# Perceiver block on one core: the feed-forward layer turned so that inner features lie on partitions, its layer norm taken apart, and the self attention's value products put ahead of the next scores

## The reference

```python
x = x + attn(layernorm(x), WQ, WK, WV, WO)        # scores, causal mask, softmax, values, WO
def ffn(x, W_fc, ln_w, ln_b, W_proj):
    h = einsum('btd,hd->bth', x, absmean(W_fc))   # 512 -> 2048, weights in {-1, 0, 1}
    h = gelu(h, approximate=False)
    h = layernorm(h, ln_w, ln_b)                  # over the 2048 inner features
    return einsum('bth,dh->btd', h, absmean(W_proj))
x = x + ffn(layernorm(x), ...)
```

## Time and profile before

| what | value |
|---|---|
| median of 3 runs | 1124.6 us (1123.21 to 1125.88) |
| profiled execution, its own time | 1122.38 us |
| its span, first to last instruction | 1120.2 us |
| granted TensorE clock, mean | 0.969 |
| busy PE, DVE, ACT, POOL | 956.8, 688.4, 453.0, 441.0 us |

### The profile page before, as it was taken

The page is one execution under the profiler, slowest core; times in us unless marked ns, Lnnn a source line. Parts: engine busy times, 40 slices in busy tenths (PEclk is TensorE's granted clock), DMA queues, the critical chain, the costliest instruction groups (busy, mean ns, idle before and its releaser), DMA issues.

```text
span 1120.2 us, 22904 instructions
## 1 busy us (share of the span) xinstructions
PE 956.8 (85%) x7466; PEld 809.4 (72%) x7466; DVE 688.4 (61%) x1352; ACT 453.0 (40%) x972; POOL 441.0 (39%) x572
## 2 busy tenths in 40 slices
PE   0898879888788888779798988889869999999996
PEld 0787757676676767668688887778647888888885
DVE  3587666766766767764545554655556665565554
ACT  2565445554455545444323232434363322322321
POOL 1354444444444444410212111111016767667663
PEclk9999999999999999979799998999879999999999
DMA  5532233221223222411534443334331111101101
GB/s 167 156 92 55 71 89 95 89 60 59 84 83 92 72 80 73 158 38 40 170 116 112 114 136 95 107 108 108 107 118 38 58 34 52 57 29 57 57 19 50
DMA packets 96769, 95.11 MB, mean 85 GB/s; under 512 B 41634, under 2 KB 58099, under 8 KB 96371
## 3 DMA queue, kind: packets, MB, share of 16 engines
q1 hardware_dynamic: 96016, 93.19, 28.3%
q10 hardware_dynamic: 578, 0.13, 0.1%
q0 software_dynamic: 32, 0.02, 0.0%
HBM read 76.45 MB, written 12.66 MB: 80 GB/s over the span
## 4 chain that ended last, share of the span: by engine, by line
PE 66%; DVE 15%; issue 10%; ACT 3%; DVEq 2%; ACTq 1%; POOL 1%; DMA 1%; SPq 0%; POOLq 0%
PE bank L244 52%; PE bank L219 9%; PE bank L240 4%; DVE f L233 3%; DVE f L507 2%; DVE f L930 2%; DVEq L74 1%; ACT f L230 1%; ACTq L74 1%; ACT f L412 1%; PE bank L529 1%; DVE f L974 1%; DVE f L470 1%; DMA f<-in_L_attn_WO_dram 1%; DVE f L641 1%
## 5 line engine op out<-in xcount | busy, mean ns | idle before, releaser
L244 PE MATMUL bank<-f,f 128*128 128x512 f32 (+3 forms) x5544 | 762.0, 312 | 62.4 <-issue 24.5
L244 PEld LDWEIGHTS bank<-f,f 128*128 128x128 f32 (+2 forms) x5544 | 596.5, 173 | 165.9 <-issue 67.6
L233 DVE TENSOR_TENSOR f<-bank,f 128x512 fp32r<-128x512 f32 x291 | 194.4, 686 | 129.9 <-ACT f L230 127.9
L219 PE MATMUL bank<-f,f 128*128 128x128 f32 x1152 | 170.3, 282 | 62.9 <-DVE f L619 28.7
L230 ACT ACTIVATE f<-bank 128x512 fp32r<-128x512 f32 x291 | 167.1, 593 | 110.3 <-PE bank L219 105.5
L219 PEld LDWEIGHTS bank<-f,f 128*128 128x128 f32 x1152 | 136.8, 145 | 90.1 <-DVE f L619 29.8
L936 POOL TENSOR_TENSOR f<-f,f 128x512 f32<-128x512 f32 x32 | 33.4, 1043 | 219.0 <-DVE f L933 219.0
L1153 ACT ACTIVATE f<-bank 128x512 f32<-128x512 f32 x64 | 38.3, 599 | 175.5 <-PE bank L244 175.5
L1176 POOL TENSOR_TENSOR f<-f,f 128x512 f32<-128x512 f32 x62 | 79.7, 1285 | 67.4 <-DVE f L1172 67.4
L468 POOL TENSOR_TENSOR f<-f,f 128x512 f32<-128x512 f32 x32 | 41.9, 1310 | 156.6 <-ACTq L74 135.2
L1178 POOL TENSOR_TENSOR f<-f,f 128x512 f32<-128x512 f32 x62 | 80.5, 1299 | 4.9
(11 more groups left out here) (88 smaller groups left out, 819.0 us busy)
## 6 DMA issues: line engine op xcount, KB each, us to landing
f<-in_ctx_dram SPq DMA_DIRECT2D x71, 256.0 KB, 2.8
f<-x_scratch SPq DMA_DIRECT2D x64, 256.0 KB, 3.0
f<-in_x_dram SPq DMA_DIRECT2D x32, 256.0 KB, 3.0
x_scratch<-f SPq DMA_DIRECT2D x32, 256.0 KB, 2.0
f<-in_L_ffn_W_fc_dram SPq DMA_DIRECT2D x32, 256.0 KB, 3.0
f<-in_L_ffn_W_proj_dram SPq DMA_DIRECT2D x32, 256.0 KB, 3.2
f<-in_ktab_dram SPq DMA_DIRECT2D x71, 64.0 KB, 2.0
f<-f SPq DMA_DIRECT2D x64, 64.0 KB, 2.4
```

Source lines behind the costliest of these rows:

```text
L219: f = lambda e, i=i, a=a: e.transpose(dst[:, i, :], a, ident[0:rows, 0:rows])
L233: return maybe("dve", lambda e: e.tensor_tensor(lo, src, hi.bitcast(F32), ALU.subtract), sem(name + "_lo"), waits, when)
L244: f = lambda e, i=i, a=a, b=b: e.matmul(dst, a, b, start=(first and i == 0), stop=(last and i == n - 1), skip_group_check=check)
```

## The change

Feed-forward. Four tiles of rows (512 rows) form a group, and there are 4 groups. `s3_h(q)` makes a strip: 128 inner features on partitions by the 512 rows of the group, again 8 matmuls of 128x512, with the weights now the stationary operand. 16 strips a group, 64 in all, one a slot from H0 = B3 - 3 on. The features stand on partitions at once, so the 256 transposes of `s3_T` go, and with them the statistics, the normalisation on DVE and the two parameter operations on POOL. The layer norm is taken apart: ACT applies Gelu and multiplies it by the feature's `ln_w` (a scalar per partition) into the high part, DVE makes the low part (`scalar_tensor_tensor`), ACT squares the Gelu, DVE adds the Gelu and POOL the square into sums over the strips (`acc`). `s3_p(q)`, two slots after `s3_h(q)`, multiplies the unnormalised strip by W_proj into four banks, one per tile of rows, which stay open over 16 strips. After a group `s3_stat` sums `acc` over partitions with 8 products of one column, DVE and POOL make mean and deviation (mean, square, variance, clamp, `inv_sqrt`, minus mean times it), and `s3_fin` (two DVE operations of 128x512 a tile) corrects the result: deviation times product, minus mean times deviation times a row of weight sums, plus a base. The weight sums are made once: `s3_wsum`, 32 DVE operations in slots H0 + 4 to H0 + 15, and `s3_wrow`, two fp32 products over 512 columns. The base, residual plus the row of W_proj times `ln_b`, is a POOL addition a tile (`s3_base`). Between groups the four open banks are copied out, two by ACT and two by DVE. The weights are widened in slots H0 - 5 to H0 - 2 and H0, H0 + 1, half on ACT and half on DVE.

Self attention. `s2_PV(i)` moves from order 4 to order 0.5 of slot s + 4, ahead of the scores of the next tile; `s2_ET` moves one slot earlier, `s2_O` about one slot earlier; the second `s2_exp` from order 4 to 4.6. `w_abs` and `w_quant` move to order 0.3, `w_T(n)` stands in the slot of its own `w_quant(n)` at order 4.5, and the 64 weight steps are spread over 58 slots in place of 62. The parameters `ln_w` and `ln_b` are loaded with 4-byte elements onto partitions in slot B2.

The removed bodies of `s3_h` to `s3_p` stand with the kernel above and are left out here.

```diff
         if n == 32:
             w_gamma()
-        else:
-            w_T(n - 1)
...
         for b in range(2):
-            at(s + 1, 3.0 + b, lambda i=i, b=b: s2_exp(i, b))
+            at(s + 1, 3.0 + 1.6 * b, lambda i=i, b=b: s2_exp(i, b))
             at(s + 2 + b, 2.7, lambda i=i, b=b: s2_PT(i, b))
-        at(s + 4, 4, lambda i=i: s2_PV(i))
+        at(s + 4, 0.5, lambda i=i: s2_PV(i))
         at(s + 4, 0, lambda i=i: res_load(i))
-        at(s + 5, 5.5, lambda i=i: s2_ET(i))
-        at(s + 6 if i else s + 8, 4.45, lambda i=i: s2_O(i))
+        at(s + 4, 5.5, lambda i=i: s2_ET(i))
+        at(s + 5 if i else s + 7, 5.6, lambda i=i: s2_O(i))
...
     for n in range(64):
-        s = B2 - 2 + (n * (4 * ni - 2)) // 64
+        s = B2 - 2 + (n * (4 * ni - 6)) // 64
         if n < 4:
             at(B2 - 1, 0.5, lambda n=n: w_load(n))
         if n < 32:
-            at(s + 3, 3.9, lambda n=n: w_abs(n))
+            at(s + 3, 0.3, lambda n=n: w_abs(n))
         else:
-            at(s + 3, 4.5, lambda n=n: w_quant(n))
+            at(s + 3, 0.3, lambda n=n: w_quant(n))
+            at(s + 3, 4.5, lambda n=n: w_T(n))
     B3 = B2 + 4 * ni
-    at(B3 - 1, 9, lambda: w_T(63))
+    H0 = B3 - 3
...
+    Gh, Gl = r[0](3, D, dt=F32R), r[1](3, D, dt=F32R)
+    sq3 = r[0](D), r[1](D)
...
     def s3_WF(n):
         src, dst = WFb[:, :, n * 512:(n + 1) * 512], WF[:, :, n * 512:(n + 1) * 512]
+        w = [*tok["qk", ni // 2 - 1], *tok["wb", 0]]
...
+            tok["WF", n] = op("act", lambda e: e.activation(dst, src, ACT.Copy), sem("f_W"), w)
...
+            tok["WF", n] = op("dve", lambda e: e.tensor_copy(dst, src), sem("f_WF0"), w)
...
+    def s3_T(i):
+        g, j = i // 4, i % 4
+        u = g % 2
+        w = d2("h", 16 * (g - 2) + 15) if g > 1 else (tW[3] if u == 0 else [tok["WF", n] for n in range(4)])
+        ln_T(ni + i, XFh[u][:, :, j * 128:(j + 1) * 128], XFl[u][:, :, j * 128:(j + 1) * 128], take(), w)
+    def s3_h(q):
+        g, f = q // NF, q % NF
+        u, y = g % 2, q % 3
+        k = take()
         terms = []
         for c in range(4):
...
+            w = WF[:, c, f * 128:(f + 1) * 128]
+            terms += [(w, XFh[u][:, c, :]), (w, XFl[u][:, c, :])]
+        rows = [t for j in range(4) for t in tok["XT", ni + 4 * g + j]]
+        tk = products(bank[k][:, :], terms, "f_h", [tok["WF", f // 4], *rows, *gfree[k]])
+        tok["h", q] = [tk]
+        tg = op("act", lambda e: e.activation(g3[:, y, :], bank[k][:, :], ACT.Gelu), sem("f_gelu"),
+                [tk, *d2("gread", q - 3)])
+        give(k, [tg])
+        th = op("act", lambda e: e.activation(Gh[:, y, :], g3[:, y, :], ACT.Copy, scale=lwp[:, f:f + 1]),
+                sem("f_G_hi"), [tg, tok["lwb"], *tok["sc", ni - 1], *d2("p", q - 3)])
+        tl = op("dve", lambda e: e.scalar_tensor_tensor(
+            Gl[:, y, :], g3[:, y, :], lwp[:, f:f + 1], Gh[:, y, :].bitcast(F32), ALU.mult, ALU.subtract),
+            sem("f_G_lo"), [th, tok["lwb"], *tok["sc", ni - 1], *d2("p", q - 3)])
+        tok["G", q] = [th, tl]
+        v = g % 2
+        if f == 0:
+            ts = op("act", lambda e: e.activation(acc[:, v, 1, :], g3[:, y, :], ACT.Square), sem("f_gelu"),
+                    [tg, *wfree[63], *d2("stat", g - 2)])
+            tok["acc2", g] = [ts]
+        else:
+            z = q % 2
+            ts = op("act", lambda e: e.activation(sq3[z][:, :], g3[:, y, :], ACT.Square), sem("f_gelu"),
+                    [tg, *tok["sc", ni - 1], *tok.get(("sqr", z), [])])
+            tp = op("pool", lambda e: e.tensor_tensor(acc[:, v, 1, :], acc[:, v, 1, :], sq3[z][:, :], ALU.add),
+                    sem("f_acc2"), [ts, *tok["acc2", g]])
+            tok["acc2", g] = tok["sqr", z] = [tp]
+        if f:
+            a = g3[:, (q - 1) % 3, :] if f == 1 else acc[:, v, 0, :]
+            ta = op("dve", lambda e: e.tensor_tensor(acc[:, v, 0, :], a, g3[:, y, :], ALU.add), sem("f_dv"),
+                    [tg, tl, *tok.get(("acc", g), []), *wfree[63], *d2("stat", g - 2)])
+            tok["acc", g] = [ta]
+            tok["gread", q] = [ta, ts]
+            if f == 1:
+                tok["gread", q - 1] = [ta, tok["sq0"], th]
+        else:
+            tok["sq0"] = ts
+    def s3_p(q):
+        g, f = q // NF, q % NF
+        if f == 0:
+            tok["kp", g] = [take() for t in range(4)]
+        kp, y = tok["kp", g], q % 3
+        for t in range(4):
+            for v, G in enumerate((Gh, Gl)):
+                fn = lambda e, t=t, v=v, G=G: e.matmul(
+                    bank[kp[t]][:, :], G[:, y, t * 128:(t + 1) * 128], WP[:, f, :],
+                    start=(f == 0 and v == 0), stop=(f == NF - 1 and v == 1))
+                w = [*(gfree[kp[t]] if f == 0 else ()), tok["WP", f // 4], *tok["G", q]]
+                tk = op("pe", fn, sem("f_p") if v else None, w if v == 0 else ())
+            tok["pt3", g, t] = [tk]
+        tok["p", q] = [tk]
+        if f == NF - 1 and g < ng - 1:
+            for t in range(4):
+                if t % 2:
+                    te = op("dve", lambda e, t=t: e.tensor_copy(Po[:, t, :], bank[kp[t]][:, :]), sem("f_dv"),
+                            [*tok["pt3", g, t], *tok["ptT", ni - 1, 1], *tok["vx", ni - 1], *d2("fin", g - 1, t)])
+                else:
+                    te = op("act", lambda e, t=t: e.activation(Po[:, t, :], bank[kp[t]][:, :], ACT.Copy), sem("f_gelu"),
+                            [*tok["pt3", g, t], *tok["ptT", ni - 1, 1], *tok["vx", ni - 1], *d2("fin", g - 1, t)])
+                tok["po", g, t] = te
+                give(kp[t], [te])
+    def s3_stat(g):
+        v, k = g % 2, take()
+        for t in range(4):
+            for z in range(2):
+                tk = op("pe", lambda e, t=t, z=z: e.matmul(
+                    bank[k][:, z * 4 + t:z * 4 + t + 1], acc[:, v, z, t * 128:(t + 1) * 128], ones[:, 0:1],
+                    start=True, stop=True, skip_group_check=True), sem("f_p") if t + z == 4 else None,
+                    [*tok["acc", g], *tok["acc2", g], *gfree[k], t_on] if t + z == 0 else ())
+        tok["stat", g] = [tk]
+        D_ = lambda f, w: op("dve", f, sem("f_dv"), w)
+        free = [t for j in range(4) for t in d2("fin", g - 1, j)]
+        t1 = D_(lambda e: e.tensor_scalar(smu[:, :], bank[k][:, 0:4], 1.0 / FF, None, ALU.mult), [tk, *free])
+        t2 = D_(lambda e: e.tensor_tensor(ssq[:, :], smu[:, :], smu[:, :], ALU.mult), [t1])
+        t3 = D_(lambda e: e.scalar_tensor_tensor(svar[:, :], bank[k][:, 4:8], 1.0 / FF, ssq[:, :], ALU.mult, ALU.subtract),
+                [t2])
+        give(k, [t3])
+        t3 = D_(lambda e: e.tensor_scalar(svar[:, :], svar[:, :], 0.0, None, ALU.max), [t3])
+        t4 = inv_sqrt("f_r3", srs[:, :], ssq[:, :], svar[:, :], 1.0, 1e-5, [t3])
+        t5 = D_(lambda e: e.scalar_tensor_tensor(snm[:, :], smu[:, :], -1.0, srs[:, :], ALU.mult, ALU.mult), [t4])
+        tok["nm3", g] = [t4, t5]
+    def s3_wsum(f):
+        src = WP[:, f, :].bitcast(F32)
+        for z, (eng, s) in enumerate((("dve", lwp), ("dve", lbp))):
+            w = [tok["WP", f // 4], tok["lwb"], *tok["pv", ni - 1], *tok.get(("wsum", z), [])]
+            if f == 0:
+                fn = lambda e, z=z, s=s: e.tensor_scalar(wsum[:, z, :], src, s[:, f:f + 1], None, ALU.mult)
+            else:
+                fn = lambda e, z=z, s=s: e.scalar_tensor_tensor(wsum[:, z, :], src, s[:, f:f + 1], wsum[:, z, :],
+                                                                ALU.mult, ALU.add)
+            tok["wsum", z] = [op(eng, fn, sem("f_dv"), w)]
+    def s3_wrow():
+        for z in range(2):
+            k = take()
+            tk = op("pe", lambda e, z=z, k=k: e.matmul(bank[k][:, :], ones[:, :], wsum[:, z, :], start=True, stop=True),
+                    sem("f_p"), [*tok["wsum", z], t_on, *gfree[k]])
+            ts = op("act", lambda e, z=z, k=k: e.activation(sums[:, z, :], bank[k][:, :], ACT.Copy), sem("f_gelu"),
+                    [tk, *tok["pv", ni - 1]])
+            give(k, [ts])
+            tok["sums"] = [ts]
+    def s3_res(i):
+        g, j = i // 4, i % 4
+        w = [tok["WP", n] for n in range(4)]
+        tok["xr3", i] = dma(xr3[:, j, :], x2d[i * 128:(i + 1) * 128, :], f"s_cx0{j}", [*tok["ost", i], *w, *d2("fin", g - 1, j)])
+    def s3_base(i):
+        j = i % 4
+        tok["xb", i] = op("pool", lambda e: e.tensor_tensor(xr3[:, j, :], xr3[:, j, :], sums[:, 1, :], ALU.add),
+                          sem("f_acc2"), [tok["xr3", i], *tok["sums"]])
+    def s3_fin(i):
+        g, j = i // 4, i % 4
+        tb = op("dve", lambda e: e.scalar_tensor_tensor(xr3[:, j, :], sums[:, 0, :], snm[:, j:j + 1], xr3[:, j, :],
+                                                        ALU.mult, ALU.add), sem("f_dv"),
+                [tok["xb", i], *tok["nm3", g]])
+        if g < ng - 1:
+            src, w = Po[:, j, :], [tok["po", g, j]]
+        else:
+            src, w = bank[tok["kp", g][j]][:, :], tok["pt3", g, j]
```

(25 more changed lines are left out.)

122 lines of the change are left out of this document (25 added, 97 removed).

## The result

The changed kernel takes 1141.4 us (median of 4 runs, 1138.1 to 1144.2) against 1123.9 us before (4 runs, 1121.7 to 1125.9): a ratio of 1.016, interval 1.0126 to 1.0195. It is 17.5 us slower where 29 us less were forecast, and outside the range. The profiled execution took 1138.14 us with a span of 1136.3 us, 16.1 us more than before; the forecast span was 1091.2, so 45.1 us have to be found.

What follows compares the result with a forecast made beforehand. PE was taken as the bound, busy 85% of the span and never idle in the steady feed-forward. Terms -28 + 7 - 18 - 12 + 12 + 10 = -29 us gave a 1095.6 us median; 8-in-10 range 1074 to 1118.

Steps and rivals of the forecast that it cites:

- A: Feed-forward strips: 64 times 0.44 us of transposes leave an all-PE chain, matmuls keep their pace; -28 us.
- B: PE work added by the fp32 products of `s3_stat` and `s3_wrow`: +7 us, between +4 and +10.
- C: Hand-over from self attention to feed-forward: fewer PE waits and less low clock, -18 us, between -10 and -22.
- D: Self attention: waits behind the normalisation go and about half of `w_T`'s 12.2 us; -12 us, between 0 and -24.
- E: Feed-forward strips: DVE and POOL taking turns make work late; +12 us, bounds 0 and +33.
- F: Tail after PE's last matmul: statistics, bases and corrections on DVE and POOL; +10 us, between +7 and +12.
- the case in which the engines overlap: Tail: DVE and POOL work at once, so DVE ends about 7.5 us behind PE, against 11.8 if they exclude each other.
- rival 3: Strips: DVE and POOL pace them at 4.7 us each, 65 us in place of 12, 1148.6 us; chance 0.06.
- Rival 2: Self attention and hand-over: DVE keeps its backlog, only the removed transposes pay; -11 us, 1113.6 us; chance 0.14.
- Rival 4: Strips: squares beside Gelu cost two table loads a strip on ACT, 45 us in place of 12, 1128.6 us; chance 0.04.

Runs made afterwards that it cites:

- e16: The changed kernel with only `w_T` moved, from order 4.5 of its quantisation's slot to order 0.2 of the next slot: 1121.8 us.
- e10: The changed kernel with squares and bias added on DVE, weighted sums over 20 slots, layer norm and weight transposes later, self attention of before: 1087.2 us.
- e15: e10 with the self attention put back into the change's own slots and orders: 1085.5 us.
- e5: The changed kernel with the 60 additions of the squares on DVE instead of POOL: 1131.0 us.
- e14: e10 with the 60 additions of the squares put back on POOL: 1100.4 us.
- e11: The changed kernel with squares on DVE, self attention of before and later layer norm transposes, without 30 of the 32 weighted sums: 1095.0 us.

## Why the prediction was wrong, step by step

- **A, transposes removed (-28): right.** There are 64 strips, and no transposes but the layer norm's. In the plain middle of groups two and three four strips mostly take 15.0 to 15.3 us, with one tile's transposes (0.44 us) among them, and the last strips of group four take 3.63 us each, 0.23 us a matmul; it costs the same with the operands' sides changed.
- **B, PE work added (+7, bound 10): too small.** The products of one column take 6.9 us instead of 5.9, 0.11 us a record from their start to that of the next work; one column is no cheaper than the row of 128 had suggested. `s3_wrow`, two products over 512 columns, takes 2.8 us to the next work instead of 0.9 to 1.8. 9.7 us in all, at the upper bound.
- **C, hand-over: right in size, but what was to show it did not appear.** 24.4 us for the slots ahead of the strips, 24 expected. PE is busy 66% of them (16.2 us) where over 80% was named, the clock there is 0.86, and PE waited 6.4 us once for a quantisation.
- **D, self attention (-12): wrong in sign, and one of the two steps that turned the result.** The 7.0 us behind the normalisation went, as said. That half of `w_T`'s waits would go with them was the failed sentence: they were 12.6 us, not 6. The split, moved early on DVE, stood directly ahead of the quantisation, and `w_T`, in the slot of its own `w_quant`, waited for it. e16 moves only `w_T` and gives 19.6 us. With it tile 14's values come at 782.7 us, 7.7 us earlier than before. That is the worth of the late `w_T` and not of the reordering: with the order of before and the late `w_T` (e10) they come at 780.5 us, and e15 and e10 are 1.7 us apart, within what medians can tell. The text named what stood ahead on DVE (masks, maxima, split) and still took half of the wait away, and its bounds had no loss in them.
- **E, DVE and POOL in the strips (+12, bound 33): right in kind, three times too small, and over its bound of 33.** In the kernel after the stretch is 28.6 us over a sum that held 12 for this term; less some 3 us for B, the term was about 38. From e16 to e15 only this is mended (additions on DVE, sums spread, transposes later): 36.3 us. Single pieces, each in its own kernel: turns 10.4 (e5) or 13.2 (e14), weighted sums 9.7 (e11). The lead was priced with `s3_p` behind `s3_h` (5.3 us), and that is nearly never waited for. `ln_T`, which had one slot behind `ln_apply`, was not in the sum at all. Nor was the clock, 0.94 in the first group, which was named as a sign of being wrong, and 0.97 later, where it had been 1.00. The step that failed is +12 "below the middle, because POOL's additions lag without anyone on PE's path waiting for them": nobody on PE's path waits for POOL's sums, but DVE's operations are slowed by the additions (0.69 to 1.58 us), and PE waits for DVE.
- **F, tail (+10): +6.4**, the case in which the engines overlap, since half of DVE's operations there read a bank.

The rivals. The slower one (rival 3, 0.06) named the mechanism, but as an even pace of 4.7 us in all groups; the strips ran at 3.75 us in the middle of the groups and lost their time in the first group and at each group's end. Rival 2 was half right: the reordering did not pay. Rival 4 did not happen: there are three table loads at the hand-over and none for the 64 squares between Gelus. That speaks against the estimate of about 1300 us that I had worked out from the Trainium skill, ScalarE: Activation LUTs, section Table sets: the hidden batching unit, whose list of functions in every set has no square.

On the turns, the Trainium skill, SBUF — State Buffer, section SBUF: two separate sides, was the better guide than my middle. It has DVE operations with two SBUF inputs, or in a two-port mode, and those of GpSimd that read SBUF exclude each other. The rows agree for POOL's 128x512 additions: 0.69 us became 1.58 beside them (1.33 on average over all), and `ln_apply` with one SBUF tile went from 0.54 (e10) to 1.48 us (1.09 on average), while operations that read a bank stayed at 0.75. They do not show it for POOL's small steps, beside which nothing slowed. By that rule alone the text had 1116.6 us.

Set the forecast's sum without E, 1083.6 us, beside e15's 1085.5: most of the gains were there. That the two are so close is in part luck: in e15 tile 14's values come 6.4 us later than forecast and the strips take 6.3 us more, and the hand-over and the tail take 4.5 us less. What was missed is what the change needed beside itself.

## What to carry to other kernels

A reordering that takes away a wait for an engine shortens nothing unless that engine's queue gets shorter too: list what stands ahead of the next operation that PE will meet, and give that one lead (one line, 19.6 us here). Slots alone do not say enough: in the kernel before `w_T` was called a slot behind its quantisation, which stood late in its slot (order 4.5), and PE waited 12.2 us for it. Elementwise work put on POOL "beside" DVE is not free when both read SBUF: 120 additions on DVE beat 60 on each by 10 to 13 us. Where extra work of an engine comes in a lump, price that stretch by itself, with every operation that reads its results and each one's lead.

## What was not expected of the hardware

- A DVE operation with one SBUF tile and two scalars per partition also slows beside POOL: `ln_apply` takes 541 ns on average in e10 and 1105 ns with POOL's additions put back (e14), that is about 537 ns away from them and 1511 ns beside them.
- The records of a plain fp32 product over 512 columns (L1258) start 0.85 to 1.02 us apart and those over one column 0.11 us, against 0.23 us for a matmul of the kernel's split product over 512 columns.
- Waits can cost more than themselves: in e14, 4.6 of 13.8 us are the same 1197 records at a mean clock of 0.98 instead of 0.99.
